# A width-3 convolution in front of blockwise attention and a gated low-rank feed-forward: from a transform with 4 products per 2 outputs, split into float32r passes, to one with 6 products per 4 outputs in native float32

## The reference, cut to what matters

```python
# x: (2, 1024, 1024) float32
x = x + attn(layernorm(x))
x = x + ffn(layernorm(x))

def attn(inputs, conv_w, conv_b, wq, bq, ...):
    # conv_w: (3, 1024, 768), three taps over the position
    x = conv(inputs, conv_w, padding='SAME') + conv_b
    q, k, v = split(x, 3)                       # 256 columns each
    # blocks of 128 positions, 16 heads of 64, causal softmax in the block
    ...
    return o @ proj_w + proj_b
```

## Time and profile before

| | before |
|---|---|
| median of 3 runs | 916.4 us (915.55 to 916.84) |
| the profiled execution | 917.03 us, of which the span is 915.3 us |
| TensorE busy | 873.6 us (95%), weight loads 726.6 us (79%) |
| VectorE busy | 439.7 us (48%) |
| ScalarE busy | 395.7 us (43%) |
| GpSimd busy | 326.3 us (36%) |
| DMA | mean 93 GB/s |

### The profile page before, as it was taken

One profiled execution on the slowest core, in us unless ns is written; L12 is line 12 of the kernel. 1 busy time (PEld: TensorE's weight loads), 2 busy tenths in 40 slices (PEclk: granted clock), 3 DMA queues, 4 the chain that ended last, 5 costly groups with the idle time before them and its releaser, 6 DMA issues.

```text
span 915.3 us, 14506 instructions
## 1 busy us (share of the span) xinstructions
PE 873.6 (95%) x5376; PEld 726.6 (79%) x5376; DVE 439.7 (48%) x1238; ACT 395.7 (43%) x1024; POOL 326.3 (36%) x295
## 2 busy tenths in 40 slices
PE   3799999998999979999999999999988999999997
PEld 3345788846888868888888888888867999999997
DVE  6944774958453333433323332433267444444442
ACT  5601332741332256867676767676674111111110
POOL 3454756548665222433343424342223100000000
PEclk9899999999999999999999999999999999999999
DMA  6145333225433332012125232020312312221211
GB/s 235 41 137 182 94 92 95 74 72 187 131 104 94 121 116 105 1 35 93 35 93 218 94 88 98 31 93 1 139 61 79 116 52 87 93 92 50 90 47 47
DMA packets 41291, 85.01 MB, mean 93 GB/s; under 512 B 9091, under 2 KB 27523, under 8 KB 40580
## 3 DMA queue, kind: packets, MB, share of 16 engines
q1 hardware_dynamic: 38916, 75.69, 25.2%
q0 software_dynamic: 2304, 8.39, 2.2%
HBM read 60.60 MB, written 23.07 MB: 91 GB/s over the span
## 4 chain that ended last, share of the span: by engine, by line
PE 88%; DVE 5%; ACT 2%; issue 2%; DMA 1%; POOL 1%; DVEq 0%; ACTq 0%
PE net_psum L62 20%; PE net_psum L63 19%; PE net_psum L64 19%; PE net_psum L913 8%; PE net_psum L997 4%; PE net_psum L1036 4%; PE net_psum L1004 4%; PE net_psum L1051 3%; PE net_psum L1052 2%; PE net_psum L1053 2%; PE net_psum L1065 2%; PE net_psum L895 1%; DVE x_lo L661 1%; PE net_psum L1121 1%; PE net_psum L906 1%
## 5 line engine op out<-in xcount | busy, mean ns | idle before, releaser
L405 POOL TENSOR_TENSOR pr<-pr,rrec 128x512 f32<-128x512 f32 x64 | 66.6, 1041 | 244.7 <-DVE rrec L708 244.7
L62 PE MATMUL net_psum<-fw_hi,xT_hi 128*128 128x354 f32 (+1 forms) x384 | 126.5, 329 | 0.0
L64 PE MATMUL net_psum<-fw_hi,xT_lo 128*128 128x354 f32 (+1 forms) x384 | 124.9, 325 | 0.0
L63 PE MATMUL net_psum<-fw_lo,xT_hi 128*128 128x354 f32 (+1 forms) x384 | 124.8, 325 | 0.0
L62 PE MATMUL net_psum<-x_hi,w_hi 128*128 128x512 f32 x288 | 114.3, 397 | 4.1 <-DVE w_lo L666 4.1
L63 PE MATMUL net_psum<-x_lo,w_hi 128*128 128x512 f32 x288 | 112.8, 392 | 0.0
L64 PE MATMUL net_psum<-x_hi,w_lo 128*128 128x512 f32 x288 | 112.7, 391 | 0.0
L715 DVE CUSTOM_DVE_ANT_0 pr<-net_psum,mask 128x128 f32<-128x128 f32 x256 | 58.8, 286 | 103.3 <-PE net_psum L997 103.3
L522 ACT ACTIVATE pr<-pr,negmax 128x128 f32<-128x128 f32 x256 | 99.0, 390 | 12.5 <-DVE negmax L715 12.5
L473 ACT ACTIVATE w_hi<-raw 128x1024 fp32r<-128x1024 f32 x36 | 38.1, 1058 | 134.9 <-PE net_psum L64 88.8
L385 POOL TENSOR_TENSOR raw<-raw 128x256 f32<-128x256 f32 x48 | 56.5, 1177 | 95.8 <-DMA raw<-in_conv_w 95.8
(11 more groups left out here) (137 smaller groups left out, 1892.6 us busy)
## 6 DMA issues: line engine op xcount, KB each, us to landing
raw<-in_conv_w SPq DMA_DIRECT2D x48, 384.0 KB, 3.7
xn<-in_x SPq DMA_DIRECT2D x16, 512.0 KB, 5.0
xr<-in_x SPq DMA_DIRECT2D x8, 1024.0 KB, 4.9
x_scratch<-xr SPq DMA_DIRECT2D x8, 1024.0 KB, 4.0
x1t<-x_scratch SPq DMA_DIRECT2D x16, 512.0 KB, 4.1
out<-y POOLq DMA_DIRECT2D x16, 512.0 KB, 5.0
c_scratch<-cy SPq DMA_DIRECT2D x12, 512.0 KB, 3.3
c_raw<-c_scratch SPq DMA_DIRECT2D x8, 768.0 KB, 4.8
```

The costliest lines, as they stand in the source:

```text
L62: pe.matmul(out, w_hi, x_hi, start=first, stop=False)
L63: pe.matmul(out, w_hi, x_lo, start=False, stop=False)
L64: return pe.matmul(out, w_lo, x_hi, start=False, stop=last)
L405: pool.tensor_tensor(pr[:, jj % 4], pr[:, jj % 4], rrec[:, jj % 4].unsqueeze(2).to_broadcast([P, UN, P]), ALU.mult).then_inc(s["p_ready"], 1)
```

## The change

The pairs become groups of four positions. The input has 6 combinations (`NV` = 6) of 256 columns (`QUADS`) for each chunk, so a stage is 8 x 6 products of 128x128 with 128x256. All of them run in native float32; the split into high and low parts and `three_pass` are gone from the convolution. Both batches' transformed inputs are resident (`u[0]`, `u[1]`).

The slots are now one chunk of one stage (`UNITS`, 96 of them). In each batch the first two stages alternate, chunk by chunk: (0,0), (0,1), (1,0), (0,2), (1,1), and so on. The raw weights come in slots of 4 chunks (24 loads of 768 KB). Loads 0 to 2 are mixed by GpSimd, the other 21 by VectorE, in place. Each stage uses 3 PSUM banks in place of 4, and two sums share one bank. `wv` is split inside the convolution, and the third attention step is moved in front of its last unit. The feed-forward keeps 3 tiles of x1 in flight in place of 4.

```diff
+    for n in range(N):
+        a, b = MC * n, MC * n + 1
+        UNITS += [(a, 0)] + [unit for c in range(DC - 1) for unit in ((a, c + 1), (b, c))] + [(b, DC - 1)]
+        UNITS += [(st, c) for st in range(MC * n + 2, MC * n + MC) for c in range(DC)]
+    LOAD_AT = {last_use(q) + 1: q + RR for q in range(NQ - RR)}
+    MIX_AT = {6: 3}
+    MIX_AT.update({12 + 4 * i: 4 + i for i in range(8)})
+    MIX_AT.update({44: 12, 47: 13, 51: 14, 57: 15, 60: 16, 64: 17})
+    MIX_AT.update({68 + 4 * i: 18 + i for i in range(6)})
+    TRANSFORM_AT = {-1: (0, (0, 1)), 0: (0, (2,)), 2: (0, (3,)), 4: (0, (4, 5)), 8: (0, (6,)), 10: (0, (7,)),
+                    29: (1, (0,)), 33: (1, (1,)), 37: (1, (2,)), 41: (1, (3,)), 45: (1, (4,)), 49: (1, (5,)), 52: (1, (6,)), 55: (1, (7,))}
+    TURN_AT = {28: 0, 31: 1, 35: 2, 39: 3, 43: 4, 46: 5, 50: 6, 53: 7}
+    EVAC_AT = {UNIT[st, DC - 1] + 1: st for st in range(STEPS)}
+    STATS_AT = {17 + j: j for j in range(LT)}
...
+            def load_raw(q):
+                st, h = LOADS[q]
+                if q >= RR:
+                    sync.wait_ge(s["unit_done"], last_use(q - RR) + 1)
+                sync.dma_start(raw[:, q % RR, :, 0:3], conv_w[st % MC, :, WQ * h:WQ * h + WQ]).then_inc(raw_loaded[q % RR], 16)
...
@@ GpSimd, loads 0 to 2
             def mix(q):
+                r = raw[:, q % RR]
+                pool.wait_ge(raw_loaded[q % RR], 16)
+                pool.tensor_tensor(r[:, :, W1], r[:, :, G0], r[:, :, G2], ALU.add)
+                pool.tensor_scalar(r[:, :, W3], r[:, :, G0], -0.25, None, ALU.mult)
+                pool.tensor_scalar(r[:, :, W4], r[:, :, G1], 0.5, None, ALU.mult).then_inc(s["first_mix_ready"], 1)
+                pool.wait_ge(s["first_mix_ready"], 4 * q + 1)
+                pool.tensor_tensor(r[:, :, W2], r[:, :, W1], r[:, :, G1], ALU.subtract)
+                pool.tensor_tensor(r[:, :, W3], r[:, :, W3], r[:, :, G2], ALU.subtract).then_inc(s["first_mix_ready"], 1)
+                pool.wait_ge(s["first_mix_ready"], 4 * q + 2)
+                pool.tensor_tensor(r[:, :, W1], r[:, :, W1], r[:, :, G1], ALU.add)
+                pool.tensor_tensor(r[:, :, W3], r[:, :, W3], r[:, :, W4], ALU.subtract).then_inc(s["first_mix_ready"], 1)
+                pool.wait_ge(s["first_mix_ready"], 4 * q + 3)
+                pool.tensor_tensor(r[:, :, W4], r[:, :, W3], r[:, :, G1], ALU.add).then_inc(s["first_mix_ready"], 1)
...
@@ ScalarE
             def evacuate(st):
-                act.activation(cy[:, :, 1], acc[st % 2][:, Q1, :], ACT.Identity, bias=cb_c[:, m:m + 1], scale=0.5).then_inc(s["p1_ready"], 1)
+                act.activation(ef[:, 0], a[:, 1, 0], ACT.Identity, bias=cb_c[:, m:m + 1], scale=-1.0 / 6.0)
+                act.activation(ef[:, 1], a[:, 1, 1], ACT.Copy, scale=-1.0 / 6.0)
+                act.activation(ef[:, 2:4], a[:, 2], ACT.Copy, scale=-1.0 / 6.0).then_inc(s["ef_ready"], 1)
...
@@ VectorE
             def transform(n, c):
+                src = xT_0[:, c] if n == 0 else xT_1[:, c % 2]
+                out = u[n][:, c]
+                d0123, d1234, d2345 = (src[:, a:a + L].rearrange("p (i b) -> p b i", b=4) for a in range(3))
+                wait(dve, s["u_ready"], DC * n + c)
+                dve.scalar_tensor_tensor(ba[:], d1234[:, 0:2], -4.0, d1234[:, 2:4], ALU.mult, ALU.add)
+                dve.tensor_tensor(diff[:, 1:3], d1234[:, 2:4], d1234[:, 0:2], ALU.subtract)
+                dve.tensor_tensor(diff[:, 0:4:3], d0123[:, 0:4:3], d2345[:, 0:4:3], ALU.subtract).then_inc(s["diff_ready"], 1)
+                dve.wait_ge(s["diff_ready"], DC * n + c + 1)
+                dve.tensor_tensor(out[:, 2], ba[:, 1], ba[:, 0], ALU.add)
+                dve.tensor_tensor(out[:, 3], ba[:, 1], ba[:, 0], ALU.subtract)
+                dve.scalar_tensor_tensor(out[:, 0:2], diff[:, 0:2], 4.0, diff[:, 2:4], ALU.mult, ALU.add)
+                dve.scalar_tensor_tensor(out[:, 4], diff[:, 1], 2.0, diff[:, 2], ALU.mult, ALU.add)
+                dve.scalar_tensor_tensor(out[:, 5], diff[:, 1], -2.0, diff[:, 2], ALU.mult, ALU.add).then_inc(s["u_ready"], 1)
+
@@ VectorE, loads 3 to 23
+            def mix(q):
+                r = raw[:, q % RR]
+                dve.wait_ge(raw_loaded[q % RR], 16 * (q // RR + 1))
+                dve.tensor_tensor(r[:, :, W1], r[:, :, G0], r[:, :, G2], ALU.add)
+                dve.scalar_tensor_tensor(r[:, :, W3], r[:, :, G0], -0.25, r[:, :, G2], ALU.mult, ALU.subtract).then_inc(s["sum_ready"], 1)
...
+                dve.scalar_tensor_tensor(r[:, :, W3], r[:, :, G1], -0.5, r[:, :, W3], ALU.mult, ALU.add).then_inc(s["mix_ready"], 1)
 
             def outputs(st):
+                dve.wait_ge(s["ef_ready"], st + 1)
+                wait(dve, s["c_stored"], 16 * st)
+                dve.tensor_tensor(sums[:], ef[:, 0:2], ef[:, 2:4], ALU.add)
+                dve.tensor_tensor(ef[:, 0:2], ef[:, 0:2], ef[:, 2:4], ALU.subtract).then_inc(s["sums_ready"], 1)
+                dve.wait_ge(s["sums_ready"], st + 1)
+                dve.scalar_tensor_tensor(cy[:, :, 0], a[:, 0, 0], 0.25, sums[:, 0], ALU.mult, ALU.add)
+                dve.scalar_tensor_tensor(cy[:, :, 3], ef[:, 1], 8.0, ef[:, 0], ALU.mult, ALU.add).then_inc(s["mixed"], 1)
+                dve.scalar_tensor_tensor(cy[:, :, 1], ef[:, 1], 2.0, ef[:, 0], ALU.mult, ALU.add)
+                dve.scalar_tensor_tensor(cy[:, :, 2], sums[:, 1], 4.0, sums[:, 0], ALU.mult, ALU.add)
+                dve.wait_ge(s["mixed"], st + 1)
+                dve.tensor_tensor(cy[:, :, 0], cy[:, :, 0], sums[:, 1], ALU.add)
+                dve.tensor_tensor(cy[:, :, 3], cy[:, :, 3], a[:, 0, 1], ALU.subtract).then_inc(s["cy_ready"], 1)
...
@@ TensorE
             def conv_slot(k):
+                if c == 0:
                     wait(pe, s["cy_ready"], st - 1)
+                if c % WQ == 0:
+                    if q < RR:
+                        pe.wait_ge(s["first_mix_ready"], 4 * q + 4)
+                    else:
+                        pe.wait_ge(s["mix_ready"], q - RR + 1)
+                if st % MC < 2:
+                    pe.wait_ge(s["u_ready"], DC * n + c + 1)
+                for v, w, b, h in PRODUCTS:
+                    mm = pe.matmul(acc[st % 2][:, b, h], raw[:, q % RR, c % WQ, w], u[n][:, c, v], start=c == 0 and h == 0, stop=c == DC - 1,
+                                   skip_group_check=True)
+                mm.then_inc(s["unit_done"], 1)
+                if k in (NU - 5, NU - 3, NU - 2):
+                    attention_step(0, (NU - 5, NU - 3, NU - 2).index(k))
```

More of the change, by code:

```diff
@@ L85, in network @@
     STEPS = MC * N
-    ORDER = [(0, 0), (0, 1), (1, 0), (0, 2), (1, 1), (0, 3), (1, 2), (1, 3)]
-    ORDER += [(st, p) for st in range(2, STEPS) for p in range(DC // 2)]
-    NK = len(ORDER)
-    AT = {pair: k for k, pair in enumerate(ORDER)}
-    NATIVE = (0, 1, MC)
-    native = [st in NATIVE for st, _ in ORDER]
-    split_no = [sum(not f for f in native[:k]) for k in range(NK)]
-    RR, WR = 3, 2
-    LAST_USE = {0: 1, 1: MC}
-    DVE_SCALES = (2, 5, LT - 1)
-    U_AT = {-1: (0, 0), 0: (0, 2), 1: (0, 4), 2: (0, 6), 21: (1, 0), 22: (1, 2), 23: (1, 4), 25: (1, 6)}
@@ L97, in network @@
[L97 to L107 removed]
+    UNITS = []
@@ new lines, in network @@
+    for n in range(N):
+        a, b = MC * n, MC * n + 1
+        UNITS += [(a, 0)] + [unit for c in range(DC - 1) for unit in ((a, c + 1), (b, c))] + [(b, DC - 1)]
+        UNITS += [(st, c) for st in range(MC * n + 2, MC * n + MC) for c in range(DC)]
+    NU = len(UNITS)
+    UNIT = {unit: k for k, unit in enumerate(UNITS)}
+    WQ = 4
+    LOADS = [load for n in range(N) for load in
+             [(MC * n + st, h) for h in range(DC // WQ) for st in range(2)] + [(st, h) for st in range(MC * n + 2, MC * n + MC) for h in range(DC // WQ)]]
@@ new lines, in network, with last_use @@
+    LOAD = {load: q for q, load in enumerate(LOADS)}
+    NQ = len(LOADS)
+    RR = 3
+    DVE_SCALES = (2, 5, LT - 1)
+    FIRST = MC * DC
+    def last_use(q):
+        st, h = LOADS[q]
+        return UNIT[st, WQ * h + WQ - 1]
+    LOAD_AT = {last_use(q) + 1: q + RR for q in range(NQ - RR)}
[3 more added lines that the diff above has]
+    MIX_AT.update({68 + 4 * i: 18 + i for i in range(6)})
@@ L109, in act_scaled @@
     def act_scaled(n, j):
         return (LT - len(DVE_SCALES)) * n + sum(i not in DVE_SCALES for i in range(j + 1))
-    def splits(k):
-        return 0 <= k < NK and not native[k]
     NG = TOK // GT
@@ L228, in network @@
+        yp = (tuple(psum[:, b] for b in (1, 2, 7)), tuple(psum[:, b] for b in (3, 4, 6)))
         x_loaded = [sp.sem(f"x_loaded{j}") for j in range(LT)]
@@ L421, in _ @@
                 power(0, j)
-            mix(0)
-            mix(1)
-            for k in range(NK - 2):
-                mix(k + 2)
-                if k in STATS_AT:
-                    power(1, STATS_AT[k])
-            pool.wait_ge(s["unit_done"], unit(STEPS - 1, 1) + 1)
+            for q in range(RR):
+                mix(q)
+            for j in range(LT):
```

(19 more changed lines are left out.)

293 lines of the change are left out of this document (106 added, 187 removed).

## The result

The changed kernel is 0.9% slower: 924.96 us median (923.43 to 925.67, 4 runs) against 916.62 (915.55 to 916.91) for the kernel before on the same chip, a ratio of 1.0091 with a 95% interval of 1.0073 to 1.0108. The forecast was 909.0 and "faster", with a range of 897 to 930 that holds the time. The profiled execution took 925.64 us for a span of 923.9.

A forecast was written before the change was run, and what follows sets the result against it. TensorE was taken as the bound (88% of the chain of waits). Convolution end at 320.9 plus a 12.5 us hand-over put `values` at 333.4, 7.4 us earlier: 916.4 - 7.4 = 909.0 us, range 897 to 930.

The forecast's parts named there:

- TensorE's work: Convolution products: 278.4 us removed, 576 native products of 256 columns at 0.216 added (248.8 us); alone a gain of 29.6 us.
- VectorE's prices: VectorE in the convolution: `mix` 3.8 us, `transform` 4.4, `outputs` 4.0, with 0.34 ns an element for the 4-float step.
- One of its own signs of being wrong: VectorE in the convolution: the forecast is wrong if strided instructions cost over 1.0 us.
- The rival of the doubled price: VectorE: the 4-float step doubles the price, `transform` 5.5 us, convolution ends at 341.1, total 930; chance 0.20.
- The start: Units 0 to 15, GpSimd and VectorE in turns: unit 0 at 37.0, unit 16 at 94.7, costing 24.4 us.
- The middle: Unit 16 to last convolution product: units 207.3 us, transposes 6.9, attention steps 5.0, waits 7; ends at 320.9.
- The hand-over: Last convolution product to first product of `values`: 12.5 us where the kernel before has 14.2.
- Free step: VectorE: the 16-byte step costs nothing, unit 16 comes 2 us earlier, lateness 4, hand-over 12; total 903; chance 0.22.
- GpSimd starves: Start: VectorE keeps the port for all transforms, mix 2 ends at 69.5, loss 5 us, total 914; chance 0.07.
- Port doesn't bind: Start: GpSimd's mixes run beside the transforms at 9.2 us each, unit 16 at about 79, total 890; chance 0.07.
- One side of the step alone: VectorE: only the reads or only the writes pay for the 4-float step, total 915 to 917; chance 0.09.
- Dearer pass: TensorE: a pass of 256 columns costs 0.229 us, about 8 us more, total 917; chance 0.04.

The follow-up runs named there:

- b1: Changed kernel with first mixes on VectorE, turns and outputs(1) later, permuted transposes making `transform` reads contiguous, four strided `outputs` writes instead of six: 889.7 us, ratio 0.9685.
- e3: Changed kernel with both the reads of `transform` and the operations of `outputs` on cy made contiguous (other numbers computed): ratio to the kernel before 0.9891.
- e1: Changed kernel with the three 4-float-step reads of `transform` made contiguous (other numbers computed): ratio to the kernel before 0.9922.
- e2: Changed kernel with all six operations of `outputs` on cy made contiguous (output positions permuted): ratio to the kernel before 1.0020.
- e7: Changed kernel plus operations run alone behind its work; VectorE reads of 512 elements: by 2 floats nothing extra, by 3 about 0.14 us, by 4 and 8 0.37 to 0.40.
- e9: Changed kernel with the two one-operand operations of a GpSimd mix given two operands (other numbers computed): ratio to the kernel before 1.0107.
- e4: Changed kernel with the mixes of the first three weight loads moved from GpSimd to VectorE: median 911.8 us, ratio to the kernel before 0.9944.
- e5: Changed kernel with batch 1's turns two slots later, its transforms two or three later, and outputs(1) in slot 19 instead of 16: ratio to the kernel before 1.0000.

## Why the prediction was wrong, step by step

**TensorE's work: right.** 144 records without a wait take 31.35 us (b1), 0.2165 apart; taken 0.216.

**VectorE's prices: the step that failed.** `mix` was right (106.45 to 110.21 us after, 3.76; taken 3.8). The step of 4 floats was taken at 0.34 ns an element from L828 and measures 0.72 to 0.78 in the reads and about 0.6 in the writes, so a `transform` was 5.2 and not 4.4, an `outputs` 4.3 and not 4.0. In the whole kernel the sum had 6 us for the step (909.0 against 903 without it); the ratios with it and without it (1.0091, and 0.9891 in e3) lie 18 us apart. So some 12 of the 16 us that the forecast was short are this term. One of its own signs of being wrong, a strided instruction of over 1.0 us, came true with 1.07. I had written down both ends and chose by the row nearest in kind. That row has 32 elements where the change has 512, one strided operand out of two, and its surcharge is 11 ns in 193: a difference of that size in one pair of rows prices nothing that is sixteen times longer. The measured price of a read lies at three quarters of the way to the doubled end. The rival of the doubled price was to decide from about 5.0 us for a `transform` and 4.5 for an `outputs`: the first was passed, the second was not. Its 930 was 5 too high, and its mechanism was what happened, with the reads carrying most of it (e1 13.2 us, e2 5.3).

The Trainium skill, "SBUF — State Buffer", under "Door 1: The DMA port swizzle", has the lines of 16 bytes that want two hits. e7 agrees: by 2 floats free, by 3 a price of 0.14 us, by 4 and 8 one of 0.37 to 0.40. Its sentence that calls a step of 4 float32 free fits no row of VectorE here; a step of 2 is the free one.

**The start: sign right, size short.** Unit 0 was forecast to 0.3 us and unit 16 missed by 3.7; the 16 first units took 61.2 us, not 58. Mix 2 was to end near 55 and ended at 62.3. Each of 24 GpSimd operations took 1.71 us between 21.2 and 62.3, where 1.41 was taken. Some 4.3 us of the 7.3 come with the strided reads: in e1 mix 2 ends at 57.95, and an operation takes 1.53. Where the other 3 us come from is open. That it is from the operations with one operand, for which I had taken 0.6 us (alone they take 1.48, e7), is what e9 speaks against.

**The middle: 11.4 us short.** VectorE idles 3.86 us for the store of stage 0, as forecast, and then works from 102.22 until the last tile is normalised at 138.35, with one gap of 0.59 us for GpSimd's power: the forecast had 131.3. Counted from unit 16, that is 39.9 us where it had 36.6. The stretch holds eight statistics where I counted seven (2 us), the gap, two `outputs` of 4.2 (0.5 us more) and a start 0.3 us later; so the wait is 7.1 us instead of 3.6. It is the sum of VectorE's work behind that store. e1 and e4 take nothing out of the stretch and leave the wait as it is, e2 and e3 take 1.8 us out and get 1.9 us back at units 20 and 28, and e5 takes the wait for the store out and moves the turn. I had the queue in the sum and never asked why its last item had to be ready then: nothing needs that turn before unit 48. The forecast saw TensorE wait for `mix` there; that wait was there too, until 135.3, under the longer one.

Behind the wait comes a part that I had left out: the units behind that wait run slower. After, 19 records from 140.17 take 6.20 us, where they would take 4.3 at the spacing above, at a granted clock of 0.66 between 140 and 146 us: 1.9 us more, and the eight transposes ahead of them 1.76 instead of 0.88. The remaining waits (units 20, 50, 58, 64 and 68) came to 7.4 us, for which 3.4 had been taken. They belong to the price of the step: in e3 only 0.3 us before unit 20 and 0.8 before unit 68 are left of them. These pieces make 10.3 of the 11.4 us; the units themselves (0.2165 for 0.216) and the attention steps (5.4 us for 5.0) have 0.9 more.

**The hand-over: right** (11.6 for 12.5). Behind it the feed-forward was taken as unchanged, and its tiles take 0.08 us more each, 0.9 us in all over twelve; no run says why.

**The rivals.** Free step: with every step taken out (e3) the ratio of 0.9891 is 906.6 us for a kernel of 916.6, against 903 forecast; the sum without the step was 4 us too low. GpSimd starves: no, it ends mix 2 at 62.3, not 69.5. Port doesn't bind: no, e4 gains 11.7 us in the start by taking GpSimd out of it. One side of the step alone (915 to 917): no, both sides pay. Dearer pass: no, 0.2165. Two sums in this part of the prediction are off without moving a chance: unit 16 at 79 is 15.7 us early and gives 893, not 890, and VectorE's work in stages 2 to 5 at the doubled price adds up to 94 us (30.4 + 27.5 + 20.4 + 16), not 96.

## What to carry to other kernels

Look at an engine's longest strided access before its count of instructions. If the trace has no row of that size and step, give the dear end of the bracket at least half of the chance instead of reading a middle value out of a small row. Where a change fills an engine, list its queue ahead of each thing TensorE waits for and ask of each item when it is really needed; doing a turn two slots and an `outputs` three slots later gave 5 us here (e5). An idle engine is no help by itself: GpSimd did three mixes in the start, and VectorE doing them on top of its own work was 12 us faster (e4).
